# Weights kept in SBUF and checked by PE and DVE, attention output transposed in 32x32 squares by DVE

## What is computed

```python
x = L0_attn_hidden_states                       # 32 x 256 x 128, that is 8192 tokens of 128 numbers
q = x @ Wq.T + bq
probs = softmax(q @ memory_keys.T / sqrt(128))  # over 4096 slots
output = probs @ memory_values @ Wo.T + bo
x = layernorm(x + output)
h = silu(tlin(x, w1)) * tlin(x, w2)             # 128 -> 512, tlin(x, w) = (x @ w.T) * s
h = gelu(tlin(h, h1)); h = gelu(tlin(h, h2))    # 512 -> 512
x = layernorm(x + tlin(h, w3))                  # 512 -> 128
```

## Time and profile before

| | us |
|---|---|
| three runs: median (lowest to highest) | 1159.92 (1159.88 to 1163.5) |
| the profiled execution's own time | 1158.77 |
| its span, first to last instruction | 1157.1 |

### The profile page before, as it was taken

How to read it: one execution, slowest core, us unless ns; L and a number is a source line. 1 busy time by engine, 2 the same in 40 slices (tenths; PEclk the granted TensorE clock), 3 DMA queues, 4 the chain that set the end, 5 groups by cost and what they waited for, 6 DMA issues and landing times. The chain is left out here.

```text
span 1157.1 us, 20319 instructions
## 1 busy us (share of the span) xinstructions
PE 1096.3 (95%) x5323; PEld 772.4 (67%) x5323; DVE 971.9 (84%) x1804; ACT 905.0 (78%) x1612; POOL 653.1 (56%) x624
## 2 busy tenths in 40 slices
PE   6899999999999999999999999487999999999996
PEld 5566666666666666666666666235788788788875
DVE  6888898998999899899999989753788888888774
ACT  6788788888878888887888886545878888887883
POOL 1487788878878887887888788370021121121110
PEclk9999999999999999999999999778999999999999
DMA  6888888888988888888889898831011001001000
GB/s 195 191 189 200 201 205 199 206 199 204 206 200 206 205 201 200 211 199 197 209 201 206 199 212 192 192 100 54 13 30 54 27 27 54 27 27 54 10 10 27
DMA packets 84514, 165.94 MB, mean 143 GB/s; under 512 B 19712, under 2 KB 48128, under 8 KB 84224
## 3 DMA queue, kind: packets, MB, share of 16 engines
q1 hardware_dynamic: 79968, 160.97, 58.6%
q10 hardware_dynamic: 4512, 4.56, 1.5%
HBM read 22.85 MB, written 8.39 MB: 27 GB/s over the span
## 5 line engine op out<-in xcount | busy, mean ns | idle before, releaser
L464 POOL TENSOR_TENSOR pT<-slot_p,pT 128x512 f16<-128x512 f32 x496 | 561.6, 1168 | 140.3 <-ACT pT L527 133.2
L527 ACT ACTIVATE pT<-slot_p 128x512 f16<-128x512 f32 x512 | 297.4, 617 | 101.1 <-DMA slot_p<-rows 81.6
L628 DVE TENSOR_SCALAR_CACHE_REDUCE rows<-s_ps 128x1024 f32<-128x1024 f32 x256 | 311.3, 1216 | 62.5 <-DMA slot_p<-rows 31.3
L597 DVE STREAM_TRANSPOSE rows<-rows 128x1024 f32<-128x1024 f32 x256 | 317.1, 1239 | 3.2 <-ACT rows L518 3.2
L518 ACT ACTIVATE rows<-rows,bias 128x1024 f32<-128x1024 f32 x256 | 291.7, 1140 | 8.1 <-DVE bias L636 8.0
L725 PE MATMUL s_ps<-keys,q_buf 128*128 128x512 f32 x512 | 250.3, 489 | 7.9 <-DVE rows L628 4.2
L699 PE MATMUL o_ps<-pT,v_hi 128*128 128x512 f16 x512 | 199.5, 390 | 29.5 <-POOL pT L464 25.9
L999 PE MATMUL ring<-h_hi,keys 128*128 128x512 f32 x512 | 205.3, 401 | 2.0 <-DVE h_lo L945 1.7
L726 PE MATMUL s_ps<-keys,q_buf 128*128 128x512 f32 x512 | 202.7, 396 | 0.0
L1000 PE MATMUL ring<-h_lo,keys 128*128 128x512 f32 x512 | 202.3, 395 | 0.0
L727 PE MATMUL s_ps<-keys,q_buf 128*128 128x512 f32 x512 | 201.7, 394 | 0.0
(11 more groups left out here) (91 smaller groups left out, 1219.3 us busy)
## 6 DMA issues: line engine op xcount, KB each, us to landing
slot_p<-rows SPq DMA_DIRECT2D x1020, 128.0 KB, 2.4
x_in<-in_xT SPq DMA_DIRECT2D x32, 128.0 KB, 2.2
x_in<-in_x SPq DMA_DIRECT2D x16, 256.0 KB, 3.3
o_scratch<-o_sum SPq DMA_DIRECT2D x32, 128.0 KB, 1.9
out<-y_out SPq DMA_DIRECT2D x16, 256.0 KB, 2.3
o_in<-o_scratch SPq DMA_DIRECT2D x14, 256.0 KB, 3.0
w_check<-in_w_all ACTq DMA_DIRECT2D x27, 108.0 KB, 2.8
slot_p<-in_vT SPq DMA_DIRECT2D x4, 512.0 KB, 9.0
```

Source lines behind the costliest of these rows:

```text
L464: nc.gpsimd.tensor_tensor(halves(s % RING, 1), slots_first(pp, s), halves(s % RING, 0), ALU.subtract).then_inc(split, 1)
L527: nc.scalar.activation(halves(s % RING, 0), slots_first(pp, s), ACT.Copy).then_inc(highed, 1)
L597: nc.vector.transpose(row_piece(tile, k), row_piece(tile, k)).then_inc(turned, 1)
L628: nc.vector.tensor_scalar(row_piece(tile, k), s_ps[:, j % 2, :], 1.0, None, ALU.mult, ALU.max, accum_out=part_max[:, tile, k:k + 1]).then_ ...
```

## The change

- The rounded weights are kept in SBUF as they are checked (`w_all`); the loads of weights in frame 32, POOL's three casts and `partition_all_reduce` go.
- The maximum over partitions: PE transposes one column (frame 31, t = 8) and DVE reduces it (j = 5); PE (before its `turn_x1` of block 0, moved from t = 11 to t = 13) waits for it. Both read the register in frame 32.
- `output_sum` is followed by a DVE transpose in 32x32 squares from `o_sum` into `o_tmp`. The store writes each partition in four runs of 64 numbers (256 bytes). `load_o` is four DMAs (one for each 32 partitions, runs of 128 numbers) that put the squares where they belong, so that `o_in` holds tokens by features.
- `turn_output` goes. `residual` reads `o_in` in SBUF where it read `y_ps` in PSUM, and waits for the loads.
- `output_half` waits for the store before (it was `output_sum` that did). SP's loads in the turns wait for the inverse deviation.
- At the start of feed-forward SP loads all raw weights (128 x 5632 numbers, 2.9 MB), which only the case of a maximum over zero reads; ACT waits for them in turn 1.
- Small tensors of attention's start move into buffers of the row stage.

```diff
+        self.w_all = sb("w_all", [P, CHECK_COLS * CHECKS], FP32R)
...
-        self.o_in = sb("o_in", [P, 2, BT], FP32)
+        self.o_in = sb("o_in", [P, 2, GROUPS, 4, G], FP32)
...
     def load_o(self, eng, b, par):
-        eng.dma_start(self.o_in[:, par, :], self.o_dram[:, bass.ds(b * BT, BT)]).then_inc(self.o_loaded[par], 16)
+        turned = self.o_dram[:, bass.ds(b * BT, BT)].rearrange("(g i) (u n) -> u i g n", g=GROUPS, u=GROUPS)
+        for u in range(GROUPS):
+            eng.dma_start(self.o_in[u * G:(u + 1) * G, par, :, :, :].rearrange("i g s j -> i g (s j)"),
+                          turned[u]).then_inc(self.o_loaded[par], 16)
...
-    def residual(self, dve, b):
-        dve.wait_ge(self.y_done, b + 1)
+    def residual(self, dve, b, par, loads):
+        dve.wait_ge(self.o_loaded[par], 16 * GROUPS * loads)
...
-            self.nc.vector.scalar_tensor_tensor(out=self.z1[:, n, :], in0=self.y_ps[:, n, :],
-                                                scalar=self.rden[:, bass.ds(4 * b + n, 1)], in1=self.xb[:, n, :],
+            self.nc.vector.scalar_tensor_tensor(out=self.z1[:, n, :].rearrange("p (g j) -> p g j", j=G),
+                                                in0=self.o_in[:, par, :, n, :],
+                                                scalar=self.rden[:, bass.ds(4 * b + n, 1)],
+                                                in1=self.xb[:, n, :].rearrange("p (g j) -> p g j", j=G),
                                                 op0=ALU.mult, op1=ALU.add).then_inc(self.z1_ready, 1)
...
     def output_half(self, act, p, par):
-        at_least(act, self.o_ready, p)
+        at_least(act, self.o_stored, 16 * p)
...
     def output_sum(self, dve, p, par):
-        at_least(dve, self.o_stored, 16 * p)
+        at_least(dve, self.o_ready, p)
...
+        dve.wait_ge(self.o_added, p + 1)
+        self.nc.vector.transpose(self.o_tmp[:, :].rearrange("p (u s j) -> p s u j", u=GROUPS, j=G),
+                                 self.o_sum[:, :].rearrange("p (s u j) -> p s u j", u=GROUPS, j=G)).then_inc(self.o_ready, 1)
 
-    def store_output(self, sp, p):
+    def store_output(self, sp, p, odd):
+        room, at = self.o_dram[:, odd * 2 * G:odd * 2 * G + TOKENS], (p - odd) * 2 * P
         sp.wait_ge(self.o_ready, p + 1)
-        sp.dma_start(self.o_dram[:, bass.ds(p * 2 * P, 2 * P)], self.o_sum[:, :]).then_inc(self.o_stored, 16)
+        sp.dma_start(room[:, bass.ds(at, BT)].rearrange("p (u n) -> p u n", u=GROUPS)[:, :, 0:2 * G],
+                     self.o_tmp[:, :].rearrange("p (u n) -> p u n", u=GROUPS)).then_inc(self.o_stored, 16)
...
-                    if is_step(f, PAIRS) and t == 0:
-                        pool.wait_ge(w_maxed, CHECKS + 1)
-                        nc.gpsimd.partition_all_reduce(low_max[:, :], low_parts[:, CHECKS:], P,
-                                                       bass.bass_isa.ReduceOp.max).then_inc(low_found, 1)
...
-            for n, (first, end, at) in enumerate(W_PARTS):
-                pool.wait_ge(stage.w_loaded[n], 16)
-                nc.gpsimd.tensor_copy(keys[:, first:end], rows[:, at:at + end - first]).then_inc(stage.w_ready, 1)
...
-                        nc.scalar.activation(w_round[:, :], w_check[:, :], ACT.Copy).then_inc(w_rounded, 1)
-                    if is_step(f, PAIRS - 2) and t == 0:
-                        for b in range(2):
-                            act.wait_ge(stage.o_stored, 16 * 2 * (b + 1))
-                            stage.load_o(act, b, b)
+                        nc.scalar.activation(check_part(f), w_check, ACT.Copy).then_inc(stage.w_rounded, 1)
+                    if is_step(f, PAIRS - 2) and t in (0, 9):
+                        act.wait_ge(stage.o_stored, 16 * 4)
+                        stage.load_o(act, t // 9, t // 9)
...
-                    if is_step(f, PAIRS) and t == 7:
-                        load_weights(act, 0)
...
+                    if is_step(f, PAIRS - 1) and j == 5:
+                        dve.wait_ge(low_turned, 1)
+                        nc.vector.reduce_max(stage.low_max[0:1, :], stage.x1_ps[0:1, 0:P], AX.X).then_inc(stage.low_found, 1)
+                    if is_step(f, PAIRS) and j == 1:
+                        dve.wait_ge(stage.low_found, 1)
+                        stage.low_of["DVE"] = dve.value_load(stage.low_max[0:1, 0:1].bitcast(I32))
...
-                    if is_step(f, PAIRS - 2) and t == 6:
-                        stage.turn_output(pe, 0, 0, 16)
-                    if is_step(f, PAIRS - 1) and t == 6:
-                        stage.turn_output(pe, 1, 1, 16)
-                    if is_step(f, PAIRS - 1) and t == 11:
+                    if is_step(f, PAIRS) and t == 0:
+                        stage.low_of["PE"] = pe.value_load(stage.low_max[0:1, 0:1].bitcast(I32))
+                    if is_step(f, PAIRS - 1) and t == 8:
+                        pe.wait_ge(w_maxed, CHECKS + 1)
+                        nc.tensor.transpose(stage.x1_ps[0:1, 0:P], low_parts[:, CHECKS:], ident[:, :]).then_inc(low_turned, 1)
+                    if is_step(f, PAIRS - 1) and t == 13:
+                        pe.wait_ge(stage.low_found, 1)
                         stage.turn_x1(pe, 0)
...
-        w_hi = keys[:, 0:W_COLS]
+        w_hi, w_lo = stage.w_all[:, 0:W_COLS], keys[:, 2 * BT:2 * BT + W_COLS]
+        raw = rows[:, 2 * SLOTS - W_COLS:]
...
         def _(sp):
-            stage.store_output(sp, PAIRS - 1)
+            sp.dma_start(raw, w_raw[:, 0:W_COLS]).then_inc(raw_loaded, 16)
+            stage.store_output(sp, PAIRS - 1, 1)
...
-                    sp.wait_ge(stage.y_done, i + 3)
-                    sp.wait_ge(stage.xb_ready, i + 3)
+                    sp.wait_ge(stage.rstd_ready[0], i + 3)
...
-            dve.wait_ge(stage.w_ready, len(W_PARTS))
-            low = dve.value_load(low_max[0:1, 0:1].bitcast(I32))
...
-                for b in rows_blocks(i):
-                    stage.turn_output(pe, b, par, 16 * i2 + 32)
...
-            low = pe.value_load(low_max[0:1, 0:1].bitcast(mybir.dt.int32))
-            with pe.If(low > 0):
+            with pe.If(stage.low_of["PE"] > 0):
```

More of the change, by code:

```diff
@@ L132, in __init__ @@
         self.bo_loaded, self.scales_loaded, self.const_ready = sem("bo_loaded"), sem("scales_loaded"), sem("const_ready")
-        self.w_loaded = [sem(f"w_loaded{n}") for n in range(len(W_PARTS))]
-        self.w_ready, self.den_ready, self.rden_ready = sem("w_ready"), sem("den_ready"), sem("rden_ready")
+        self.w_rounded, self.den_ready, self.rden_ready = sem("w_rounded"), sem("den_ready"), sem("rden_ready")
+        self.low_found = sem("low_found")
+        self.low_of = {}
         self.o_loaded = [sem("oo_loaded0"), sem("oo_loaded1")]
         self.x_loaded = [sem("xx_loaded0"), sem("xx_loaded1")]
-        self.xb_ready, self.y_done, self.z1_ready = sem("xb_ready"), sem("y_done"), sem("z1_ready")
+        self.xb_ready, self.z1_ready = sem("xb_ready"), sem("z1_ready")
         self.stats_ready = [sem("stats1_ready"), sem("stats2_ready")]
@@ L211, in split_x1 @@
         self.nc.vector.tensor_tensor(self.x1_lo, src, self.x1_hi.bitcast(FP32), ALU.subtract).then_inc(self.x1_split, 1)
[L213 to L218, removed]
     def turn_x1(self, pe, b):
@@ L377, in send @@
                               row_piece(tile, k)[g * G:(g + 1) * G, :]).then_inc(sent[tile][k], 16)
-        def load_weights(eng, n):
-            first, end, at = W_PARTS[n]
-            for c in range(at // PIECE, (at + end - first - 1) // PIECE + 1):
-                eng.wait_ge(sent[c // PIECES][c % PIECES], 16 * GROUPS * PAIRS)
-            eng.dma_start(rows[:, at:at + end - first], w_all[:, first:end]).then_inc(stage.w_loaded[n], 16)
         block_ctx = ctx.enter_context(nc.Block())
@@ L424, in frame @@
                     p, tile, k = turned_piece(f, j)
-                    if is_step(f, PAIRS) and j == PIECES:
-                        for n in (1, 2):
-                            load_weights(sp, n)
-                    elif valid(p, PAIRS):
+                    if valid(p, PAIRS) and not (is_step(f, PAIRS) and j == PIECES):
                         exchange(p, par if j > PIECES else 1 - par, tile, k)
                     if j == 3 and valid(f - 3, PAIRS) and not is_step(f, PAIRS + 2):
-                        stage.store_output(sp, f - 3)
+                        stage.store_output(sp, f - 3, 1 - par)
                     if j == 6 and valid(f + 2, PAIRS):
@@ L914, in _ @@
         def _(dve):
-            dve.wait_ge(stage.w_ready, len(W_PARTS))
-            low = dve.value_load(low_max[0:1, 0:1].bitcast(I32))
-            with dve.If(low > 0):
-                for first, end, at in W_PARTS:
-                    last = nc.vector.tensor_tensor(w_lo[:, first:end], rows[:, at:at + end - first],
-                                                   w_hi[:, first:end].bitcast(FP32), ALU.subtract)
-                last.then_inc(w_split, 1)
+            with dve.If(stage.low_of["DVE"] > 0):
```

(8 more changed lines are left out.)

79 lines of the change are left out of this document (36 added, 43 removed).

## The result

| | before | after |
|---|---|---|
| runs of the comparison: median (lowest to highest), us | 1159.9 (1159.88 to 1163.5) | 1147.64 (1145.54 to 1148.59) |
| the profiled execution's own time, us | 1158.77 | 1148.24 |
| its span, us | 1157.1 | 1146.5 |

The changed kernel is faster: the ratio of the times is 0.9884, with a 95% interval of 0.986 to 0.9908. The forecast of 1147 for the median was 0.6 us off. The terms of its sum were not that good, as the traces show.

What follows compares the result with a forecast made beforehand. Attention was taken as bound by PE (busy 624.3 of 630 us), turns by PE's chained products, with slack in frame 32. -16.8 + 2.2 + 2.7 - 0.5 - 0.5 = -12.9 gave 1145.9, median 1147, range 1139 to 1157.

Steps and rivals of the forecast that it cites:

- Point 1: Frames 32 and 33: without the all-reduce POOL goes on earlier, and the engines meet at 766.7, not 783.5: -16.8 us.
- point 2: Frames 30 and 31: block 0's residual held by POOL, and more loads on ACT's queue: +2.2 us, bounds 0 and +4.
- Point 3: Frames 3 to 29: DVE's transpose hidden, the store's short runs cost 0.2 a pass: +2.7 us, bounds 0 and +19.
- rival A: Frames 3 to 29: stores delay the last piece's landing, 1164 at 0.75 us a frame; chance 0.07, a milder form 0.14.
- The frame of 22.0 us: Attention: a frame takes 22.0 us and can't get much shorter; 22.1 to 22.2 was expected after the change.
- Point 4: Start of feed-forward: DVE's and PE's register loads go, against SP's 2.9 MB load: -0.5 us, bounds -1.2 and +4.
- The collision: Start of feed-forward: PE's code may come late if it shares the DMA engines with SP's 2.9 MB load; up to +4.
- a gap of 7 or more: Sign of being wrong: an issue gap of 7 us or more at the start of feed-forward.
- Point 5: Turns: PE's four transposes go, but PE then waits for DVE's first `prod` (0.59 us a turn): -0.5 us.
- Rival B: Turns: PE's wait for `prod` moves with PE, so 14 x 0.44 = 6.2 us are gained, time 1141; chance 0.1.
- Rival C: Tail: another wait replaces POOL's, low clock over the whole last pair (+10) or late sends: 1155 to 1157; chance 0.1.
- signs of being right: Among them: feed-forward 12 to 17 us earlier, `residual` instructions over 3 in frames 30 and 32, a frame 22.1 to 22.2.

Runs made afterwards that it cites:

- run 1: The changed kernel with its output part taken back, so only the weights part (weights kept in SBUF, no all-reduce) remains: 1144.03 us, ratio 0.9855.
- run 9: The changed kernel with block 2's four loads of `o_in` and its `x_in` load moved behind the meeting of the engines: 1143.25 us, ratio 0.9842.
- Run 4: The changed kernel with the store in 128 runs of 1 KB instead of 512 of 256 bytes: 1147.74 us, ratio 0.9883.
- run 5: The changed kernel without DVE's transpose in `output_sum`, the sums stored unturned: 1148.99 us, ratio 0.9909.
- Run 6: The changed kernel with four unread PE transposes per turn put back where `turn_output` stood: 1147.3 us, ratio 0.9886.
- run 7: The changed kernel with four unread PE transposes per turn, placed behind the product that waits for `prod`: 1153.44 us, ratio 0.9931.

## Why the prediction was right, and where it wasn't

**Point 1, the tail: right in mechanism, mis-sized.** It foretold -16.8 until the engines meet. Measured is -13.0 from the projection to the release, of which point 2 takes +0.6, so -13.6. POOL's gaps went as foretold, and the clock stayed up, so that a part costs 10.02 / 16 = 0.63 on DVE and 0.65 on PE, as taken. What was off stands at its start and its end. The times that follow are measured from the last pair's projection, and without point 2's 0.6, to stand beside the sum's. DVE began its parts at 754.1 (757.16 - 2.5 - 0.6) where the sum had it begin at 753.5, since ACT's four sends, beside SP's own, landed after up to 4.8 us and not 2.4. Its 16 parts then took 10.0 for the sum's 10.4. SP's store went out at 766.0 (769.11 - 2.5 - 0.6) where the sum had 763.9: behind the last part (767.18) DVE still has four normalisations, the sum of the pair before and its transpose, 1.9 until the store. The sum let the store follow at once, though there are 1.5 in the kernel before already, from 763.91 + 15.97 = 779.88 to 781.33. And from the store to the release 3.8 us passed for 2.1 before, where the sum had 2.8; its own terms, 2.1, three issues of 0.4 and a transpose of 0.45, add up to 3.75. Together 0.6 - 0.4 + 1.9 + 1.0 = 3.1, which is the shortfall but for rounding. The loads' part of the last term is shown by other runs: from store to release it is 2.0 in run 1, which has one load of `o_in` there, and 1.0 in run 9, which has no load at all.

**Point 2, frames 30 and 31: too dear.** +2.2 was foretold. The hold came, 2.35 and 3.28 for 1.08. But POOL's first low part of the last but one pair stands 38.16 us behind the projection for 37.53 before, so +0.6. The same distance is 37.2 to 38.1 in the four kernels without the output part and 38.1 to 38.5 in the nine with it, 0.6 more in the mean. So of the hold in frame 30 and the loads beside it 0.6 shows, and the rest is hidden. In frame 32 the hold is hidden: DVE starts its low parts 58.29 us after the projection in the changed kernel and 58.24 in run 1, since it waits for ACT and the sends there.

**Point 3, frames 3 to 29: the step that failed.** The prediction put it as "I take 0.2 a pass, near the low end": +2.7, and the profiles differ by +2.5. That the two agree is chance. Run 4 took away the small runs and run 5 the transposes, and nothing became faster; over 13 profiles the frames don't depend on the output part. The term is 0 within about 1.5 us, by the spread of these profiles, and its rival A has no ground: a landing of 2.1 for 1.9 isn't seen by the sends, whose median is 2.4 before and after. The frame of 22.0 us was wrong too: from pair 3 on the projections are 22.1 to 23.5 apart, 22.61 in the mean before and 22.64 after.

**Point 4, the start of feed-forward: the wrong sign.** -0.5 was foretold, and from the release to PE's first product it is +0.2. The register loads went, 0.6 on DVE and as much on PE, but PE's branch took 4.99 for 3.60. The collision that the text named as the upper bound, up to +4, is real: PE's code does come by the same DMA engines, and the branch takes 5.0 to 7.6 with the load at that moment and 3.4 to 3.8 with it later. So the sign that the text gave for it, a gap of 7 or more, is met in four of the six kernels, though not in this profile of the changed one. Without the load the change has its half microsecond (3.6 to 4.0 from memset to first product for 4.35 to 4.80 in kernels that have no such load).

**Point 5, the turns: right.** From PE's first product to the end it is -0.3, foretold -0.5. PE waits 0.48 for `prod` where the text had 0.59. Run 6 shows that the transposes stood in a wait, run 7 what they would be worth elsewhere. Rival B (-6.2) had mixed up a row in the chain with a row that sets the time.

**The sum.** Measured +2.5 - 13.6 + 0.6 + 0.2 - 0.3 = -10.6 between the spans (1157.1 and 1146.5), foretold -12.9; without the +2.5 of chance -13.1. The medians differ by 12.3. So where the gain comes from was seen rightly, but that the number came within 1 us is luck: a tail 3.2 too good and a start of feed-forward 0.7 too good were made up by 4.3 of costs in points 2 and 3 that aren't there. Rival C (a low clock over the last pair) fell with the granted clock of 1.00 there. Of the signs of being right three didn't come: feed-forward starts 10.5 earlier and not 12 to 17, block 0's residual took 2.35 and not over 3, and a frame is as long as before.

Open stays why the packet with PE's code starts after 2.6 us in one execution and after 5.3 in another, with the load ordered at the same place, and what POOL does in the 7 us behind the all-reduce. I also did not try the held residual with other operands, since it is hidden here.

## What to carry to other kernels

An instruction that moves off an engine is worth its time only where that engine doesn't wait next: look for the first wait behind it in the chain, and put dummy copies before and behind that wait if in doubt. The one cross-partition reduction on POOL cost 11 us in this full pipeline, though the profile gives it 0.38 us: POOL stood still on both sides of it. A column transposed by PE and reduced by DVE took its place, in run 1 with no cost that can be seen. What a queue still has to issue before all engines meet, and a large load ordered as an engine branches into new code, lie on the path: in the changed kernel both together were worth 6.8 us, over half as much as the change itself, for moving a few lines.

## What was not expected of the hardware

- A 2816 KB load ordered at the meeting lengthens PE's branch into the next part from 3.4 to 3.8 us to 5.0 to 7.6 us, though PE needs nothing of the load: a 16 KB packet of instructions stands behind it.
- Stores in 512 runs of 256 bytes land in 2.1 us, in 128 runs of 1 KB in 1.9 to 2.0, at a DMA share of 0.88.
- After the all-reduce POOL stands for 7.15 to 7.44 us, longer than before it (5.67), as far as the profile's rough spans on POOL tell.
- Up to the last projection the profiled executions lie between 695.55 and 700.04 us, without order by kernel, while the medians of the kernel before in three batches agree within 0.1%. So a term of 2 us can't be read from a pair of profiles, only from many or from an experiment.
